# A fused four-layer convolution kernel, last layer: GpSimd adds the strip before the borders, and adds the borders in two parts

## The reference

```python
y = jnp.einsum('oc,bchw->bohw', w_in, x)                    # 48 -> 288 channels
f = jnp.fft.rfft2(8x8 patches of y) * fft_mask              # per channel
y = jnp.fft.irfft2(f)
y = lax.conv_general_dilated(y, w_dw, padding=1, groups=288) # 3x3, per channel
x1, x2 = jnp.split(y, 2, axis=1)
g = jax.nn.gelu(x1) * x2
return jnp.einsum('oc,bchw->bohw', w_out, g)                # 144 -> 48 channels
```

## Time and profile before

| what | us |
|---|---|
| median of 3 runs | 11938.39 (11927.18 to 11943.02) |
| profiled execution, its own time | 11946.39 |
| its span | 11944.6 |
| last stage, in the profile | about 9450 to the end |

### The profile page before, as it was taken

How to read it: one execution, slowest core, us unless ns; L and a number is a source line. 1 busy time by engine, 2 the same in 40 slices (tenths; PEclk the granted TensorE clock), 3 DMA queues, 4 the chain that set the end, 5 groups by cost and what they waited for, 6 DMA issues and landing times. The chain is left out here.

```text
span 11944.6 us, 374350 instructions
## 1 busy us (share of the span) xinstructions
PE 11372.6 (95%) x155430; PEld 7933.0 (66%) x155430; DVE 7033.3 (59%) x16042; ACT 5102.7 (43%) x10598; POOL 4884.2 (41%) x4142
## 2 busy tenths in 40 slices
PE   8999999989998999899999999999999899889988
PEld 7877544489996777555555555555555577777776
DVE  0000355544444544588888888888888666656665
ACT  0000111134343334355555555555555567767766
POOL 0000122211340025466666666666666444444444
PEclk9999999999998999899999999999999999999999
DMA  4333466597695468866666666666666333333333
GB/s 140 130 133 132 123 160 159 153 159 140 116 163 156 149 178 228 164 85 89 88 88 88 88 88 88 88 88 88 88 89 88 91 104 106 105 96 105 107 103 94
DMA packets 2387653, 1411.49 MB, mean 118 GB/s; under 512 B 1889330, under 2 KB 2260809, under 8 KB 2313245
## 3 DMA queue, kind: packets, MB, share of 16 engines
q1 hardware_dynamic: 2111384, 1290.01, 53.5%
q10 hardware_dynamic: 275072, 105.14, 3.8%
HBM read 646.26 MB, written 449.27 MB: 92 GB/s over the span
## 5 line engine op out<-in xcount | busy, mean ns | idle before, releaser
L1795 PE MATMUL l_m<-l_wa,l_pix 128*128 128x288 f32 x8192 | 2211.2, 413 | 2.7 <-DVE l_wb L1977 2.7
L1795 PEld LDWEIGHTS l_m<-l_wa,l_pix 128*128 128x128 f32 x8192 | 1475.3, 190 | 688.6 <-issue 361.6
L1651 POOL TENSOR_TENSOR l_qkv<-l_qkv,l_copies 128x576 f32<-128x576 f32 x1024 | 1437.1, 1403 | 631.0 <-DVE l_qkv L1988 620.2
L1641 POOL TENSOR_TENSOR l_pix<-l_raw 128x516 f32<-128x516 f32 x1024 | 1217.3, 1189 | 1042.1 <-DVE l_t L2025 1017.2
L1476 PE MATMUL l1h_ps<-l1h_ring,l1h_w 96*96 96x256 f32 x6120 | 1327.3, 379 | 61.5 <-ACT l1h_ring L1418 58.6
L1476 PEld LDWEIGHTS l1h_ps<-l1h_ring,l1h_w 96*96 96x96 f32 x6120 | 998.9, 163 | 389.7 <-issue 58.8
L1509 DVE SCALAR_TENSOR_TENSOR l1h_ring<-l1h_ps,l1h_bias,l1h_columns 96x256 f32<-96x256 f32 x1020 | 670.7, 658 | 677.3 <-PE l1h_ps L1476 671.6
L509 PE MATMUL l0a_rows<-l0a_x 128*49 128x245 f32 x8144 | 1044.2, 371 | 0.0
L870 PE MATMUL l0b_bank<-l0b_x,l0b_w 49*64 49x512 f32 x9216 | 1001.0, 593 | 4.4 <-DVE l0b_w L896 4.4
L1890 ACT ACTIVATE l_ks<-l_f 94x384 f32<-94x384 f32 x1024 | 498.0, 486 | 842.8 <-PE l_f L1810 842.8
L1810 PE MATMUL l_f<-l_qkv,l_a 64*94 64x384 f32 x4096 | 834.7, 483 | 1.6 <-POOL l_qkv L1651 1.5
(11 more groups left out here) (275 smaller groups left out, 21684.5 us busy)
## 6 DMA issues: line engine op xcount, KB each, us to landing
l0a_x<-x_px_dram SPq DMA_DIRECT2D x128, 1176.0 KB, 5.2
l_edge<-l_turn SPq DMA_DIRECT2D x384, 236.2 KB
l0b_x<-x_in_dram SPq DMA_DIRECT2D x128, 493.8 KB
l_raw<-l_raw SPq DMA_DIRECT2D x128, 483.6 KB, 7.3
l_raw<-x_dram SPq DMA_DIRECT2D x1270, 48.0 KB, 3.7
l_out<-x_dram SPq DMA_DIRECT2D x264, 192.0 KB, 3.6
x_dram<-l0b_out ACTq DMA_DIRECT2D x256, 193.5 KB, 3.1
out_dram<-l_out SPq DMA_DIRECT2D x516, 96.0 KB, 2.0
```

Of the source, the lines that this page charges most:

```text
L1641: nc.gpsimd.tensor_tensor(pix[:, n % 2, i, half * HALF:(half + 1) * HALF].rearrange("p (r w) -> p r w", w=PW), in0, in1, op).then_inc(pix_ ...
L1651: nc.gpsimd.tensor_tensor(q, q, copies[:, g % 2, 1:2, :].broadcast_to([128, 2, OUTC]), ALU.add)\
L1795: last = nc.tensor.matmul(bank[i][:, 0:OUTC], pix[:, k, i, first:first + 128], wa[:, b, i, :], start=True, stop=(i in (1, 2)))
```

## The change

On GpSimd the strip is added first, before the wait for the border transfers. The borders are then added in two instructions, picture rows 0 to 3 and rows 4 to 9, each of which raises `edged` by one; `edged` therefore counts two for each unit, and its waits change with it. `gelu(u, 0)` waits for the first part alone and `gelu(u, 1)` for the second. The wait for `saved` of unit u - 3 at the strip sum goes, since the unit begins with a wait for `saved` of all units before.

```diff
@@ move_edges
                 if u >= 2:
-                    sp.wait_ge(edged, u - 1)
+                    sp.wait_ge(edged, 2 * u - 2)
@@ gelu(u, h)
+                act.wait_ge(edged, 2 * u + h + 1)
                 if h == 0:
-                    act.wait_ge(edged, u + 1)
                     act.wait_ge(carried, u + 1)
@@ GpSimd, one unit
                     nc.gpsimd.memset(turn[HI:HI + 2, u % 2, 0], 0.0).then_inc(parted, 1)
-                    pool.wait_ge(edge_in[u % 2], 32 * moves(u))
                     pool.wait_ge(parted, u + 1)
-                    nc.gpsimd.memset(edge[HI:HI + 2, u % 2, 0], 0.0).then_inc(ended_edge, 1)
-                    pool.wait_ge(ended_edge, u + 1)
-                    nc.gpsimd.tensor_tensor(tile[:, 1:9:7], tile[:, 1:9:7], edge[:, u % 2], ALU.add).then_inc(edged, 1)
-                    pool.wait_ge(edged, u + 1)
                     if ty == 0:
                         pool.sem_inc(carried, 1)
                     else:
-                        pool.wait_ge(saved, u - 2)
                         nc.gpsimd.tensor_tensor(tile[:, 1:9, 0:2 * C], tile[:, 1:9, 0:2 * C], strip[:, j], ALU.add)\
                             .then_inc(carried, 1)
                     pool.wait_ge(carried, u + 1)
+                    pool.wait_ge(edge_in[u % 2], 32 * moves(u))
+                    nc.gpsimd.memset(edge[HI:HI + 2, u % 2, 0], 0.0).then_inc(ended_edge, 1)
+                    pool.wait_ge(ended_edge, u + 1)
+                    for rows_of in (slice(0, 4 * C), slice(4 * C, EDGE)):
+                        beside = tile[:, 1:9:7, rows_of]
+                        nc.gpsimd.tensor_tensor(beside, beside, edge[:, u % 2, :, rows_of], ALU.add).then_inc(edged, 1)
+                    pool.wait_ge(edged, 2 * u + 2)
                     pool.sem_inc(mixing, 1)
                     nc.gpsimd.tensor_copy(strip[:, j], tile[:, 1:9, 8 * C:10 * C]).then_inc(saved, 1)
```

More of the change, by code:

```diff
@@ L2626, in slab @@
                         pool.sem_inc(ended_edge, 1)
-                        nc.gpsimd.tensor_copy(tile[:, 1:9, 0:C], strip[:, j, :, 0:C]).then_inc(edged, 1)
-                        pool.wait_ge(edged, u + 1)
+                        nc.gpsimd.tensor_copy(tile[:, 1:9, 0:C], strip[:, j, :, 0:C]).then_inc(edged, 2)
+                        pool.wait_ge(edged, 2 * u + 2)
                         pool.sem_inc(carried, 1)
```

## The result

The changed kernel takes 11809.32 us (median of 4 runs, 11801.49 to 11813.18) against 11939.04 before: a ratio of 0.9892 (95% interval 0.9875 to 0.9909), 130 us faster. Measured twice more beside other kernels, it was 107 and 128 us faster than before (ratios 0.9907 and 0.9887). One of the eight executions of the kernel before beside the last of these was a slow one (13173 us, granted clock 0.87 in place of 0.98) and is left out of every figure here.

A forecast was written before the change was run, and what follows sets the result against it. TensorE, busy 95%, was taken as the bound, so only its waits could move the time. Gains of 41 + 17 + 27 + 5 = 90 us gave a forecast of 11850 us, range 11815 to 11905.

The forecast's parts named there:

- Strip sum hidden in the transfer's wait: GpSimd, each unit: the strip sum (0.08 + 1.82 us) fits inside the border transfers' wait with at least 1.2 to spare.
- Price of the split: GpSimd border sum: two parts cost 0.2 us more a unit, bounded by 0 and 0.5, behind gelu's first half.
- Chain of j = 0: From transfer landing to transposes: gates done when project ends, TensorE's wait vanishes; 0.7 of 58 us returns, 41 us.
- Residual: VectorE's residual starts 1.7 us earlier, so convolve j = 2 waits less: half of 33 us, 17 us.
- The gate of j = 1: VectorE's second gate after channels slips in behind the first border part of j = 2: 27 us, ends 0 and 68.
- coin's toss: Whether that second gate is asked for inside the first border part, gaining 1.4 us, or later, gaining next to nothing; half each.
- the 0.8: Share of the second gate's saved VectorE time that was taken to reach TensorE.
- Long exposures: End of the program and last slab of the first picture pair: chain 2.4 us shorter in each, 5 us.
- the first (no opening): Rival: GpSimd runs both border parts without letting VectorE in, gate term nothing; 63 us gain, 11875; chance 0.30.
- The second (all slabs win, 11821): Rival: nearly every second gate falls into the first border part, 54 us in place of 27; 117 us gain; chance 0.14.
- The third: Rival: time comes back elsewhere, in ScalarE's copies or TensorE's pauses; 17 us gain, 11921; 0.10 together with another rival.
- the fourth: Rival: slower, both gates of j = 1 get stuck behind the two border parts; 35 us slower, 11973; chance 0.04.

The follow-up runs named there:

- j = 0 alone: Changed order and split only in units j = 0, other units as before the change; 11855.48 us, ratio 0.9928, 85 us faster than the kernel before.
- the kernel without the split: Changed kernel with the strip sum first but the border sum in one instruction; 11859.07 us, ratio 0.9932, 81 us faster than the kernel before.
- the hold alone: Kernel before, plus one wait: GpSimd's border sum of j = 2 waits until both gates of j = 1 are done; 11899.70 us, ratio 0.9965.
- j = 2 alone: Changed order and split only in units j = 2, other units as before the change; 11913.86 us, ratio 0.9978, 26 us faster than the kernel before.
- other traffic: Changed kernel plus one unneeded DRAM transfer of about 0.8 MB in each slab of the last stage; 11901.64 us, ratio 0.9964.

## Why the prediction was right and wrong

- **Strip sum hidden in the transfer's wait**: right, 1.83 inside a wait that is 452 us in place of 753.
- **Price of the split**: forecast 0.2 us a unit; the two parts take 2.39 where the one sum takes 2.23. Right.
- **Chain of j = 0**: forecast that the gates are done when `project` ends, in spite of standing behind GpSimd. Right, 10107.88 against 10108.2, and the wait went from 66.3 to 10.3. The step that failed is the sentence "Not all of it comes back": I took 0.7 of 58 us from the slower `project` in the earlier trace rows, 41 us. The stretches show 59 us for `project` and the transposes of j = 0. The slab in rows 11 had been read as a law. From its first to its last start `project` takes over 5.2 us in 13 of the 61 slabs before and in 9 after, with means of 5.03 and 4.97: so a slow `project` did not take the place of the wait. In nine of the 13 the wait was under 0.2 us, and the sum of the waits had left it out already; there was nothing to discount. The 58 us were also read a little wrong: they hold a wait of 6.5 in the very first slab and one of 5.9 at the end of the first picture pair, which the forecast's 5 us count again; in the 61 slabs they are 44 us.
- **Residual**: forecast 17 us as half of 33; the waits went altogether and convolve j = 2 became 23 us shorter. j = 0 alone, which is these two terms together, gave 85 us and not 58. The half rested on ScalarE's copies being next in line; no profile with the new order in j = 0 shows 1 us of waits for them in that stretch.
- **The gate of j = 1**: the mechanism was right, the size was not. Forecast was 27 us, from half the slabs and 0.8 of the excess. The coin's toss itself was fair: 36 of 62 gates are asked for inside the first part (medians: the landing 5.40 after the copies, the end of the first part 6.98, the gate 6.85). What was wrong is "asked later, it stands behind the second and gains next to nothing": it is stuck for the rest of a sum of 1.4, not of 2.2, and takes 1.73, not 2.22. So the excess over 0.95 fell from 1.08 to 0.49 a slab, by more than half. The stretches show 45, 36 and 38 us in the three profiles; the kernel without the split is 26 to 49 us slower. Whether the 0.8 was too high stays open: the hold alone passed on 0.6 of the excess that it took away (40 of 67 us), j = 2 alone 0.6 by the medians and 0.9 by the profiles, and the full change about all of it (36 to 45 of 37).
- **Long exposures**: forecast 5 us; TensorE's waits at the end of the first picture pair and of the program went from 5.9 and 8.1 to 3.0 and 3.1 us, 8 in all.
- **Rivals**: the first (no opening) is refuted by the gate that went in between two parts. The second (all slabs win, 11821) was the nearest, for another reason: the two terms of j = 0 came in full. The third is refuted by j = 0 alone, the fourth by the first gates of j = 1, which stay at 0.96. Every gate shown agrees with the exclusive lock of the Trainium skill ("SBUF — State Buffer", "SBUF: two separate sides"), held for the whole instruction by whichever starts first. What the Trainium skill says of a GpSimd core going on to the next instruction by itself ("GPSIMD Engine Reference", "Instruction dispatch") let me suspect that there might be no opening, and the trace shows one.

The three discounts were taken one after another, each downwards and two of them from a single slab, and the range was then built from the discounted values: its lower end, 123 us under the median, left the undiscounted sum, 58 + 33 + 54 + 5 = 150 us, outside. The 90 us were 40 short of the 130: about 18 in the chain of j = 0, 6 in the residual, 9 to 18 in the gate and 3 in the exposures. The first and second measurement of the change differ by 23 us, and their profiles by 24 us of TensorE's pauses, so about that much of the first result need not be the change's own. By the second, 107 us, the range would have held, but by luck: there too `project` and the transposes of j = 0 became 52 us shorter and convolve j = 2 20, where 41 and 17 were forecast.

## What to carry to other kernels

When two engines exclude each other for the length of an instruction, look where the short instruction that others wait for meets a long one that nobody waits for; hold the long one back with a semaphore, or cut it. Here the wait alone gave 40 us with no other edit. Count a wait that shows in nearly every period of a steady loop in full (it came back at 0.93 in j = 0; with the hold, 40 us came of 54 us of idle time), until a profile row shows what else is late by the same amount. A slower neighbour in one period is no such row: the sum of the waits has already left out the periods that had none.

## What the runs showed of the hardware

- A VectorE sum of two SBUF tensors and a GpSimd sum take turns by whole instructions, and VectorE gets its turn between two GpSimd instructions that follow each other without a wait: the gate of 0.95 took 1.36, and the two parts, 2.39 by themselves, 3.11. Of 62 gates 36 were asked for inside the first part, and took 1.32 on average.
- TensorE's unexplained pauses inside unbroken runs of products are waits for its own instructions, as far as times can show it: in the profile of before, 143 of 146 pauses of more than 0.25 us in convolve and `channels` end 1.0 to 2.0 us after a transfer of the instruction queue (16 KB each, 494 in the last stage) has landed, where random moments would give about 28. Four of the 146 have an engine that explains them; the other 142 all end 1.2 to 1.7 us after such a landing. With other traffic they were fewer and longer, 161 in place of 180 and in sum 144 us in place of 108, for 20% more GB/s (126 in place of 105); that is one profile of each.
- The changed kernel gained 107, 128 and 130 us in three measurements on different occasions, while runs within one agree to about 10 us: two variants that were not measured side by side can't be told apart by 20 us.
